# A decoder layer on one core: other places in SBUF for TensorE's operands, and an accumulation moved ahead of a row maximum

## The chip, the cores and the metric

The kernel runs on one core of a Trainium2 chip. The time is the device time of one execution in microseconds (us); of several executions the median counts.

## What is computed

A decoder layer for 8 sequences of 128 tokens, 512 features, all in float32. Cut to what matters:

```python
x = x + attn(layernorm(x))         # 32 query heads of 128 on 8 key/value heads; 16 cached blocks of 32 keys
                                   # and 128 new ones: 640 keys, rope, softmax, output projection 4096 -> 512
x = x + xattn(layernorm(x), ctx)   # rmsnorm, 32 heads of 128, keys and values from ctx (8 x 128 tokens),
                                   # score + position bias, mask, softmax, output projection 4096 -> 512
x = x + ffn(layernorm(x))          # gelu(x W1 + b1) W2 + b2, 512 -> 2048 -> 512
```

## The kernel before, in words

**Products.** A float32 product is made of three matmuls in the type float32r: each operand is split into a rounded part `_hi` (ScalarE copies, L485) and the rest `_lo` (VectorE or GpSimd subtract), and `mm3` (L1112 to L1116) adds hi x hi (L1114), hi weights x lo moving (L1115) and lo weights x hi moving (L1116). Every matmul loads its own weights. In the rows a matmul is written as output<-moving operand,weights. The trace has a row for a matmul (PE) and one for the load of its weights (PEld).

**Stages.** Three long loops follow one another, each over units of one head (or one 128-wide slice of the hidden layer) and one half of the 1024 tokens: 64 units of self-attention (`a_step`), 64 of cross-attention (`c_step`), 32 of the feed-forward part (`f_step`). Every engine runs the same list of units in an order written out by hand; semaphores tie them. The loads of the weights (SyncE) run two heads ahead.

**A unit n of self-attention on TensorE.** Scores of unit n+1 (L1179: weights q, moving K, 320 columns), queries of unit n+2 (12 products of 512 columns), then for each of 5 key tiles: four transposes of the probabilities (L1244: moving `ident`, weights `prob`), three matmuls of the output projection of unit n-1 (`a_out`: weights oT, moving wo) and three of probabilities times V (`pv`: weights V, moving pT). VectorE takes the row maxima, the low parts and the sums into `xacc` (L884).

**A unit n of cross-attention on TensorE** (L1341 to L1404), in this order: transposes of `xprob` (L1371); scores of unit n+1 (L1312, L1313: weights xq, moving xk, 256 columns); in two units of four (u mod 4 = 0, 3) a first tile of values (24 matmuls: weights cT, moving xwv, 256 columns); output product 0 of unit n-1 (`o(0)`: weights xoT, moving xwo); 12 of queries of unit n+2 (weights xwq, moving xT); in the same two units a second tile of values; `o(1)`; the product with xV (L1396, L1397: weights xV, moving xpT); 12 of keys of unit n+2 (weights xwk, moving cT); `o(2)`, `o(3)`. `o(i)` writes a bank that VectorE's accumulation i-1 (L884, `acc(i-1)`) must have emptied: `o(1)` waits for `acc(0)`.

**The same unit on VectorE** (L999 to L1049): low part of the transposed probabilities (L1010); `c_score` for unit n+1: two additions (L985, L987) and the row maximum (L990); in the two units with values a low part (L957); `acc(0)`; reciprocal (L1025); low part of the queries (L1028), which waits for ScalarE's xq_hi; factor (L1031); in the units with values the second low part; `acc(1)`; sum of the output halves (L1037); xoT_lo (L1042), which waits for ScalarE's xoT_hi; low part of the keys (L966), which waits for ScalarE's xk; `acc(2)`, `acc(3)`. ScalarE's exponentials (L631, four a unit) wait for the maximum, and its xq_hi stands behind them.

**Places.** A tensor's place is its first byte in each partition. Tensors are placed one behind the other in the order of their declaration (L50 to L137), each size rounded up to 32 bytes; a stage's tensors start again where the ones common to all end. Four names, of which the kernel reads nothing, only fill (`shift2`, `shift3`, `shift4`, 32 bytes each). All rows of the operands are a multiple of 512 bytes long or start at one, but for K (its second half starts 1280 bytes on). Places modulo 512 in the kernel before:

| operands | place before |
|---|---|
| xT, ident | 128 |
| K, q, wq, V, wo | 320 |
| prob, pT, oT, xwv | 384 |
| cT, xwk, xwq, xwo | 320 |
| xq, xk, xV, xprob, xpT, xoT | 384 |
| w1, w2 | 320 |
| hid_hi, hid_lo | 384 |

Of the kernel before, what the change touches and what calls it, by code (L numbers as in the profile page):

```python
# [13 lines left out]
P = 128  # L14
# [20 lines left out]
def decoder_layer(nc, x, ctxT, mask, fcos, fsin, wq, wk, wv, wo, kc, vc, bidx,  # L35
# [3 lines left out]
    with ExitStack() as ctx:  # L39
        def sb(stack, name, shape, dt=F32):  # L40
            return stack.enter_context(nc.sbuf_tensor(name, shape, dt))
# [14 lines left out]
        negmax = sb(ctx, "negmax", [P, 2, 4])  # L56
        rowsum = sb(ctx, "rowsum", [P, 2, 4])
        rinv = sb(ctx, "rinv", [P, 2, 4])
        sb(ctx, "shift2", [P, 8])


        with ExitStack() as ph:
            K_all = sb(ph, "K_all", [P, KB, NKV, BLOCK])
            V_all = sb(ph, "V_all", [P, KT, NKV * P])
            K_hi, K_lo = pair(ph, "K", [P, 2, T])
            q_hi, q_lo = pair(ph, "q", [P, 2, HALF])
            wq_raw = sb(ph, "wq_raw", [P, 2, C, P])
            wq_cos = sb(ph, "wq_cos", [P, C, P])
            wq_sin = sb(ph, "wq_sin", [P, C, P])
            wq_rot = sb(ph, "wq_rot", [P, C, P])  # L70
            wq_hi, wq_lo = pair(ph, "wq", [P, 2, C, P])
            V_hi, V_lo = pair(ph, "V", [P, 2, KT, P])
            wo_raw = sb(ph, "wo_raw", [P, 2, D])
            wo_hi, wo_lo = pair(ph, "wo", [P, 2, D])
            rope = sb(ph, "rope", [P, 2, P])
            ropeq = sb(ph, "ropeq", [P, 2, P])
            idx_sb = sb(ph, "idx_sb", [1, TOPK], I32)
            with ExitStack() as pro:
                kv_raw = sb(pro, "kv_raw", [P, 4, C, D])
                knew = sb(pro, "knew", [P, 3, D])  # L80
                xn1 = sb(pro, "xn1", [P, B, D])
                x0T = sb(pro, "x0T", [P, C, P])
            with ExitStack() as lo_:
                prob = sb(lo_, "prob", [P, 2, 4, T])
                pT_hi, pT_lo = pair(lo_, "pT", [P, KT, HALF])
                oT_hi, oT_lo = pair(lo_, "oT", [P, HALF])

                xwv_raw = sb(lo_, "xwv_raw", [P, C, 2 * P])
                xwv_hi, xwv_lo = pair(lo_, "xwv", [P, C, 2 * P])

        with ExitStack() as ph:

            cT_hi, cT_lo = pair(ph, "cT", [P, C, TOK])
            c_raw = sb(ph, "c_raw", [P, 2, TOK])

            xwk_raw = sb(ph, "xwk_raw", [P, 2, C, P])
            xwk_hi, xwk_lo = pair(ph, "xwk", [P, 2, C, P])
            xwq_raw = sb(ph, "xwq_raw", [P, 2, C, P])
            xwq_hi, xwq_lo = pair(ph, "xwq", [P, 2, C, P])
            bias_sb = sb(ph, "bias_sb", [P, 2, P])  # L100
            mask_sb = sb(ph, "mask_sb", [P, B, P], U8)
            negmask = sb(ph, "negmask", [P, B, P])
            lnw_sb = sb(ph, "lnw_sb", [P, D])

            xwo_raw = sb(ph, "xwo_raw", [P, 2, D])
            xwo_hi, xwo_lo = pair(ph, "xwo", [P, 2, D])
            anykey = sb(ph, "anykey", [P, B])
            sb(ph, "shift3", [P, 8])
            comb = sb(ph, "comb", [P, 2, 4, P])
            xq_hi, xq_lo = pair(ph, "xq", [P, 2, HALF])  # L110
            xk = sb(ph, "xk", [P, 2, 4, 2, P], F32R)
            xV_hi, xV_lo = pair(ph, "xV", [P, 2, 4, 2 * P])
            with ExitStack() as pro:
                xn2 = sb(pro, "xn2", [P, B, D])
            with ExitStack() as lo_:
                xprob = sb(lo_, "xprob", [P, 2, 4, P])
                xscore = sb(lo_, "xscore", [P, 2, 4, P])
                xpT = sb(lo_, "xpT", [P, 4, 2, P], F32R)
                xo = sb(lo_, "xo", [P, 2, 4, P])
                xoT_hi, xoT_lo = pair(lo_, "xoT", [P, 2, HALF])  # L120

        with ExitStack() as ph:

            w1_raw = sb(ph, "w1_raw", [P, 2, C, P])
            w1_hi, w1_lo = pair(ph, "w1", [P, 2, C, P])
            w2_raw = sb(ph, "w2_raw", [P, 2, D])
            w2_hi, w2_lo = pair(ph, "w2", [P, 2, D])
            b1_sb = sb(ph, "b1_sb", [P, 2])
            sb(ph, "shift4", [P, 8])
            b2_sb = sb(ph, "b2_sb", [P, D])  # L130
            hid = sb(ph, "hid", [P, 2, HALF])

            hid_hi, hid_lo = pair(ph, "hid", [P, 2, HALF])
            xn3 = sb(ph, "xn3", [P, B, D])
            yacc = sb(ph, "yacc", [P, B, D])
            finite = sb(ph, "finite", [P, B, D], I32)
            ysum = sb(ph, "ysum", [P, B, D])  # L137
# [11 lines left out]
        for p in (1, 2, 3):  # L149
# [17 lines left out]
        c = {n: sem("c_" + n) for n in (  # L167
            "qwhi", "qwlo", "kwhi", "kwlo", "vwhi", "vwlo", "owhi", "owlo", "comb", "S", "score", "max", "exp",
            "tr", "pThi", "pTlo", "pv", "ohi", "osum", "oThi", "oTlo", "q", "qhi", "qlo", "k", "khi", "klo", "v", "vhi", "vlo",
            "rinv", "wo", "y", "res")}  # L170
# [582 lines left out]
        def _(dve):  # L753
# [225 lines left out]
            xq_lo_evac(0, 1)  # L979
            ln_lo(2, 1)  # L980

            def c_score(n, slot, half):
                dve.wait_ge(c["S"], n + 1)
                dve.wait_ge(c["comb"], n + 1)
                v.tensor_tensor(xscore[:, slot], XS_bank[:, :, 0:P], comb[:, half], ALU.add).then_inc(c_s1, 1)  # L985
                dve.wait_ge(c_s1, n + 1)
                v.tensor_tensor(xscore[:, slot], XS_bank[:, :, P:2 * P], xscore[:, slot], ALU.add)\  # L987
                 .then_inc(c["score"], 1)
                dve.wait_ge(c["score"], n + 1)
                v.tensor_reduce(negmax[:, slot, :], xscore[:, slot], AX_X, ALU.max, negate=True)\  # L990
                 .then_inc(c["max"], 1)
# [7 lines left out]
            def c_step(it, u):  # L999
                n, k = it * 4 + u, u % 2  # L1000
                static = isinstance(n, int)
                more1, more2 = (not static or n + 1 < UNITS), (not static or n + 2 < UNITS)
                first = static and n == 0

                def acc(i):
                    if not first:
                        accumulate(c, n - 1, 1 - k, 1 - k, i, (XW_last if static and not more2 else XW_bank)[i], None)

                dve.wait_ge(c["pThi"], n + 1)
                v.tensor_tensor(xpT[:, :, 1, :], XT_bank.rearrange("p (t n) -> p t n", t=4), xpT[:, :, 0, :],  # L1010
                                ALU.subtract).then_inc(c["pTlo"], 1)
                if more1:
                    c_score(n + 1, 1 - k, 1 - k)
                vs = (u % 4 == 0 and not first) or (u % 4 == 3 and more1)
                if vs:
                    vhalf = 1 if u % 4 == 0 else 0
                    cnt = (it + u // 4) * 4 + (2 if vhalf else 4)
                    v_evac(vhalf, 0, cnt + 1)
                if not first:
                    dve.wait_ge(c["rinv"], n)  # L1020
                acc(0)
                if not static or n > 1:
                    dve.wait_ge(c["y"], 4 * n - 4)
                dve.wait_ge(c["exp"], 4 * n + 4)
                v.reciprocal(rinv[:, k, :], rowsum[:, k, :]).then_inc(c_r1, 1)  # L1025
                if more2:
                    dve.wait_ge(c["qhi"], n + 3)
                    v.tensor_tensor(xq_lo[:, k], XQ_bank, xq_hi[:, k], ALU.subtract).then_inc(c["qlo"], 1)  # L1028
                dve.wait_ge(c_r1, n + 1)

                v.tensor_tensor(rinv[:, k, :], rinv[:, k, :], anykey[:, 4 * k:4 * k + 4], ALU.mult)\  # L1031
                 .then_inc(c["rinv"], 1)
                if vs:
                    v_evac(vhalf, 1, cnt + 2)
                acc(1)
                dve.wait_ge(c["ohi"], n + 1)
                v.tensor_tensor(xo[:, 1], XO_bank[:, :, P:2 * P], xo[:, 0], ALU.add)\  # L1037
                 .then_inc(c["osum"], 1)
                if not more1:
                    acc(2)  # L1040
                dve.wait_ge(c["oThi"], n + 1)
                v.tensor_tensor(xoT_lo[:, k].rearrange("p (t n) -> p t n", t=4), xo[:, 1],  # L1042
                                xoT_hi[:, k].rearrange("p (t n) -> p t n", t=4),
                                ALU.subtract).then_inc(c["oTlo"], 1)
                if more2:
                    xk_lo_evac(k, n + 3)
                if more1:
                    acc(2)
                acc(3)  # L1049
# [467 lines left out]
```

## Time and profile before

| | |
|---|---|
| three runs | 2090.53, 2092.18, 2090.71 us; median 2090.71 |
| the profiled execution | 2089.98 us |
| its span, first to last instruction | 2088.0 us, 33806 instructions |
| granted TensorE clock, mean | 0.995 |

The span is what the profile's page and the trace cover; 1.98 us of the profiled execution lie outside it. A busy share is the time in which at least one instruction of the engine runs. The ends of TensorE's matmuls are modelled and overlap the next one's start, so the pace is read from the starts.

### The profile page before, as it was taken

How to read it: one execution, taken by the hardware profiler on the slowest of the kernel's cores; microseconds unless marked ns; L12 is line 12 of the kernel's file. 1: busy time of each engine (PE TensorE's matmuls, PEld its weight loads, DVE VectorE, ACT ScalarE, POOL GpSimd, SP SyncE). 2: the span in 40 equal slices, each digit the busy share in tenths (PEclk: the TensorE clock that was granted, in tenths of full speed). 3: DMA queues.
4: the chain of work that ended last, by engine and by line, in shares of the span. 5: the costliest groups of instructions: out<-in, count | busy, mean ns of one | idle time of the engine just before them, and what ended most of it. 6: DMA issues, size and time to landing. Idle time of an engine off the chain costs nothing.

```text
span 2088.0 us, 33806 instructions
## 1 busy us (share of the span) xinstructions
PE 2043.8 (98%) x11544; PEld 1768.8 (85%) x11544; DVE 1471.1 (70%) x2367; ACT 1012.9 (49%) x2230; POOL 530.7 (25%) x428
## 2 busy tenths in 40 slices
PE   8999999999999999999899999999999999989996
PEld 6888888888888888887788888888888888877885
DVE  6777777777777777777766666666666666677776
ACT  3555555555555555555544444444444444433331
POOL 2222212222122212222122222222222222223223
PEclk9999999999999999999999999999999999999998
DMA  7000000000000000011111111111111111011111
GB/s 233 21 21 21 21 11 20 20 20 11 19 20 20 15 15 20 15 55 32 47 43 44 43 43 43 43 43 43 43 38 37 37 43 43 23 36 27 49 48 48
DMA packets 44162, 76.90 MB, mean 37 GB/s; under 512 B 7378, under 2 KB 13650, under 8 KB 43602
## 3 DMA queue, kind: packets, MB, share of 16 engines
q1 hardware_dynamic: 44114, 76.25, 11.9%
q8 instruction: 32, 0.52, 0.1%
q14 instruction: 16, 0.13, 0.0%
HBM read 74.13 MB, written 2.10 MB: 37 GB/s over the span
## 4 chain that ended last, share of the span: by engine, by line
PE 93%; DVE 3%; ACT 2%; SPq 1%; issue 1%; DMA 0%; POOL 0%; DVEq 0%; ACTq 0%
PE bank L1114 23%; PE bank L1116 23%; PE bank L1115 23%; PE bank L1179 11%; PE bank L1244 7%; PE bank L1312 1%; PE bank L1396 1%; PE bank L1397 1%; PE bank L1313 1%; PE bank L1371 1%; PE bank L1169 0%; DVE xn L805 0%; SPq L214 0%; DVE xT_lo L811 0%; SPq L215 0%
## 5 line engine op out<-in xcount | busy, mean ns | idle before, releaser
L884 DVE SCALAR_TENSOR_TENSOR xacc<-bank,rinv,xacc 128x512 f32<-128x512 f32 x512 | 376.2, 746 | 71.4 <-PE bank L1116 71.0
L485 ACT ACTIVATE pT_hi<-bank 128x512 fp32r<-128x512 f32 x320 | 191.3, 599 | 213.0 <-PE bank L1244 213.0
L874 DVE TENSOR_REDUCE negmax<-bank 128x1 f32<-128x640 f32 x256 | 210.6, 822 | 46.6 <-PE bank L1179 39.1
L939 DVE TENSOR_TENSOR pT_lo<-bank,pT_hi 128x512 fp32r<-128x512 f32 x320 | 218.1, 682 | 2.4 <-ACT pT_hi L485 2.4
L537 ACT ACTIVATE prob<-bank,negmax 128x640 f32<-128x640 f32 x256 | 203.2, 794 | 24.5 <-DVE negmax L874 24.5
L1244 PE MATMUL bank<-ident,prob 128*128 128x128 f32 x1280 | 191.2, 272 | 0.0
L1244 PEld LDWEIGHTS bank<-ident,prob 128*128 128x128 f32 x1280 | 159.2, 140 | 19.5
L382 POOL TENSOR_TENSOR wo_lo<-wo_raw,wo_hi 128x512 fp32r<-128x512 f32 x32 | 42.1, 1315 | 413.4 <-ACT wo_hi L485 413.4
L631 ACT ACTIVATE xprob<-xscore,negmax 128x128 f32<-128x128 f32 x256 | 100.1, 394 | 95.0 <-DVE negmax L990 95.0
L1114 PE MATMUL bank<-xwv_hi,cT_hi 128*128 128x256 f32 x512 | 141.7, 277 | 1.4 <-DVE xV_lo L957 1.4
L1116 PE MATMUL bank<-xwv_hi,cT_lo 128*128 128x256 f32 x512 | 141.5, 276 | 0.0
L1115 PE MATMUL bank<-xwv_lo,cT_hi 128*128 128x256 f32 x512 | 141.4, 276 | 0.0
L1114 PE MATMUL bank<-pT_hi,V_hi 128*128 128x512 f32 x320 | 127.3, 398 | 2.5 <-DVE pT_lo L939 2.5
L382 POOL TENSOR_TENSOR xwo_lo<-xwo_raw,xwo_hi 128x512 fp32r<-128x512 f32 x32 | 41.3, 1290 | 346.5 <-ACT xwo_hi L485 346.5
L1116 PE MATMUL bank<-pT_hi,V_lo 128*128 128x512 f32 x320 | 126.8, 396 | 0.0
L1115 PE MATMUL bank<-pT_lo,V_hi 128*128 128x512 f32 x320 | 125.7, 393 | 0.0
L1179 PE MATMUL bank<-K_hi,q_hi 128*128 128x320 f32 x512 | 123.9, 323 | 1.0 <-ACT prob L537 1.0
L1114 PE MATMUL bank<-wo_hi,oT_hi 128*128 128x512 f32 x256 | 122.4, 478 | 2.0 <-DVE oT_lo L879 2.0
L1028 DVE TENSOR_TENSOR xq_lo<-bank,xq_hi 128x512 fp32r<-128x512 f32 x62 | 42.9, 692 | 108.3 <-ACT xq_hi L485 108.3
L1088 DVE TENSOR_TENSOR yacc<-bank,yacc 128x512 f32<-128x512 f32 x128 | 85.0, 685 | 47.0 <-PE bank L1116 46.8
L1179 PE MATMUL bank<-K_hi,q_lo 128*128 128x320 f32 x512 | 117.3, 310 | 0.0
L378 POOL TENSOR_TENSOR wq_lo<-wq_rot,wq_hi 128x512 fp32r<-128x512 f32 x32 | 41.7, 1302 | 293.7 <-ACT wq_hi L485 293.7
(172 smaller groups left out, 5754.3 us busy)
## 6 DMA issues: line engine op xcount, KB each, us to landing
wq_raw<-in_wq SPq DMA_DIRECT2D x32, 256.0 KB, 2.7
wo_raw<-in_wo SPq DMA_DIRECT2D x32, 256.0 KB, 2.7
xwv_raw<-in_xwv SPq DMA_DIRECT2D x16, 512.0 KB, 3.5
xwk_raw<-in_xwk SPq DMA_DIRECT2D x32, 256.0 KB, 3.6
xwq_raw<-in_xwq SPq DMA_DIRECT2D x32, 256.0 KB, 3.5
xwo_raw<-in_xwo SPq DMA_DIRECT2D x32, 256.0 KB, 2.7
w_raw<-in_w SPq DMA_DIRECT2D x32, 256.0 KB, 2.6
xacc<-in_x SPq DMA_DIRECT2D x8, 256.0 KB, 5.8
```

The source lines that it names most:

```text
L485: return s.activation(dst, src, ACT.Copy)
L537: s.activation(prob[:, slot, i, :].rearrange("p (a t) -> p a t", a=2), S_bank[i % 2], ACT.Exp, bias=negmax[:, slot, i:i + 1], scale=1.0, a ...
L631: s.activation(xprob[:, slot, i, :], xscore[:, slot, i, :], ACT.Exp, bias=negmax[:, slot, i:i + 1], scale=1.0, accum_out=rowsum[:, slot, i ...
L874: v.tensor_reduce(negmax[:, slot, i:i + 1], S_bank[i % 2], mybir.AxisListType.XY, ALU.max, negate=True).then_inc(a["max"], 1)
L884: v.scalar_tensor_tensor(xacc[:, 4 * half + i, :], M, rinv[:, k, i:i + 1], xacc[:, 4 * half + i, :], ALU.mult, ALU.add).then_inc(sems["y"], 1)
L939: v.tensor_tensor(pT_lo[:, j, :], T_bank[j % 2 if k == 0 else (j + 1) % 2], pT_hi[:, j, :], ALU.subtract).then_inc(a["pTlo"], 1)
L1088: v.tensor_tensor(yacc[:, t, :], Y_bank[i], yacc[:, t, :], ALU.add).then_inc(f["acc"], 1)
L1114: t.matmul(dst, w[0], m[0], start=start, stop=False)
L1115: t.matmul(dst, w[0], m[1], start=False, stop=False)
L1116: return t.matmul(dst, w[1], m[0], start=False, stop=stop)
L1179: last = t.matmul(S_bank[i % 2][:, hf, :], w[:, k, cols], K[m][:, ks, hf * TH:(hf + 1) * TH], start=(j == 0), stop=(j == 2))
L1244: last = t.transpose(T_bank[j % 2 if k == 0 else (j + 1) % 2][:, i * P:(i + 1) * P], prob[:, k, i, j * P:(j + 1) * P], ident[:, :])
```

## The change

Two edits. The first only moves tensors. `shift2` grows from 32 to 352 bytes, `shift1` (448 bytes) and `ahead3` (64 bytes) are new, `shift3` and `shift4` grow from 32 to 480 bytes. After it the places modulo 512 are:

| operands | before | after |
|---|---|---|
| xT, ident | 128 | 128 |
| K, q, wq, V, wo | 320 | 128 |
| prob, pT, oT | 384 | 128 |
| xwv | 384 | 192 |
| cT, xwk, xwq, xwo | 320 | 128 |
| xq, xk, xV, xprob, xpT, xoT | 384 | 128 |
| w1, w2 | 320 | 128 |
| hid_hi, hid_lo | 384 | 128 |

The second edit reorders VectorE in cross-attention: in the units without a tile of values (two of four) `acc(0)` with its wait for the factor stands between the second score addition and the row maximum, where it stood behind the maximum. In the units with values nothing moves.

```diff
-        sb(ctx, "shift2", [P, 8])
+        sb(ctx, "shift2", [P, 88])
...
             idx_sb = sb(ph, "idx_sb", [1, TOPK], I32)
+            sb(ph, "shift1", [P, 112])
...
+                sb(lo_, "ahead3", [P, 16])
                 xwv_raw = sb(lo_, "xwv_raw", [P, C, 2 * P])
...
-            sb(ph, "shift3", [P, 8])
+            sb(ph, "shift3", [P, 120])
...
-            sb(ph, "shift4", [P, 8])
+            sb(ph, "shift4", [P, 120])
...
-            def c_score(n, slot, half):
+            def c_score(n, slot, half, ahead=None):
...
                  .then_inc(c["score"], 1)
+                if ahead:
+                    ahead()
                 dve.wait_ge(c["score"], n + 1)
                 v.tensor_reduce(negmax[:, slot, :], xscore[:, slot], AX_X, ALU.max, negate=True)\
...
+                vs = (u % 4 == 0 and not first) or (u % 4 == 3 and more1)
+
+                def first_acc():
+                    if not first:
+                        dve.wait_ge(c["rinv"], n)
+                    acc(0)
+
                 if more1:
-                    c_score(n + 1, 1 - k, 1 - k)
-                vs = (u % 4 == 0 and not first) or (u % 4 == 3 and more1)
+                    c_score(n + 1, 1 - k, 1 - k, None if vs else first_acc)
                 if vs:
                     vhalf = 1 if u % 4 == 0 else 0
                     cnt = (it + u // 4) * 4 + (2 if vhalf else 4)
                     v_evac(vhalf, 0, cnt + 1)
-                if not first:
-                    dve.wait_ge(c["rinv"], n)
-                acc(0)
+                if vs or not more1:
+                    first_acc()
```

## Rows read from the trace of the kernel before

**Rows 1.** The page: busy time by engine; the chain that ended last, by engine.

```profile
PE 2043.8 (98%) x11544; PEld 1768.8 (85%) x11544; DVE 1471.1 (70%) x2367; ACT 1012.9 (49%) x2230; POOL 530.7 (25%) x428
...
PE 93%; DVE 3%; ACT 2%; SPq 1%; issue 1%; DMA 0%; POOL 0%; DVEq 0%; ACTq 0%
```

**Rows 2.** Busy time in stretches: stretch, us, engines in order, granted clock, DMA.

```profile
core 0: us, PE busy (x) PEld busy (x) DVE busy (x) ACT busy (x) POOL busy (x), PEclk, DMA share, GB/s
...
60.00:960.00 900.00, 899.72 (x5058) 787.82 (x5057) 665.54 (x1004) 498.27 (x1009) 198.85 (x179) 1.00 0.07 20
...
1030.00:1865.00 835.00, 829.48 (x4937) 726.01 (x4938) 548.97 (x938) 388.38 (x995) 232.07 (x170) 1.00 0.13 41
...
1900.00:2060.00 160.00, 160.00 (x690) 129.28 (x689) 118.14 (x145) 51.81 (x85) 38.31 (x28) 1.00 0.16 43
```

**Rows 3.** Timeline, PE, cross-attention keys, first and last of six: start us, us.

```profile
1102.28 0.39 PE L1114 MATMUL bank<-cT_hi,xwk_hi 128*128 128x512 f32 x1
...
1103.41 0.39 PE L1116 MATMUL bank<-cT_hi,xwk_lo 128*128 128x512 f32 x1
```

**Rows 4.** Timeline, PE: an output product's end, queries, first and last of seven.

```profile
1106.90 0.40 PE L1116 MATMUL bank<-xwo_hi,xoT_lo 128*128 128x512 f32 x1
1107.14 0.40 PE L1114 MATMUL bank<-xT_hi,xwq_hi 128*128 128x512 f32 x1
...
1108.54 0.40 PE L1114 MATMUL bank<-xT_hi,xwq_hi 128*128 128x512 f32 x1
```

**Rows 5.** Groups of PE, shapes apart: xcount | busy us, mean ns | idle before.

```profile
L1115 PE MATMUL bank<-pT_lo,V_hi 128*128 128x512 f32 x320 | 125.7, 393 | 0.0
...
L1115 PE MATMUL bank<-wo_lo,oT_hi 128*128 128x512 f32 x256 | 101.3, 396 | 0.0
L1115 PE MATMUL bank<-xwo_lo,xoT_hi 128*128 128x512 f32 x256 | 101.3, 396 | 0.0
...
L1115 PE MATMUL bank<-xT_lo,xwq_hi 128*128 128x512 f32 x256 | 100.8, 394 | 0.0
L1115 PE MATMUL bank<-xT_lo,wq_hi 128*128 128x512 f32 x256 | 100.4, 392 | 0.0
...
L1115 PE MATMUL bank<-cT_lo,xwk_hi 128*128 128x512 f32 x256 | 100.2, 391 | 0.0
...
L1115 PE MATMUL bank<-xT_lo,w_hi 128*128 128x512 f32 x128 | 50.5, 395 | 0.0
```

**Rows 6.** The same view: transposes, values and the product with xV.

```profile
L1244 PE MATMUL bank<-ident,prob 128*128 128x128 f32 x1280 | 191.2, 272 | 0.0
...
L1115 PE MATMUL bank<-xwv_lo,cT_hi 128*128 128x256 f32 x512 | 141.4, 276 | 0.0
...
L1396 PE MATMUL bank<-xpT,xV_hi 128*128 128x256 f32 x256 | 63.7, 282 | 0.0
```

**Rows 7.** Timelines of one cross-attention unit (u mod 4 = 2): VectorE, weight load, matmul.

```profile
1108.47 0.69 DVE L990 TENSOR_REDUCE negmax<-xscore 128x4 f32<-128x512 f32 x1
1109.07 0.74 DVE L884 SCALAR_TENSOR_TENSOR xacc<-bank,rinv,xacc 128x512 f32<-128x512 f32 x1
...
1109.87 0.19 PEld L1114 LDWEIGHTS bank<-xwo_hi,xoT_hi 128*128 128x128 f32 x1 [0.20 <-DVE xacc L884]
...
1109.94 0.43 PE L1114 MATMUL bank<-xwo_hi,xoT_hi 128*128 128x512 f32 x1
```

**Rows 8.** The unit's waits on VectorE (timeline); one of PEld (waits: total, times, longest).

```profile
1111.37 0.69 DVE L1028 TENSOR_TENSOR xq_lo<-bank,xq_hi 128x512 fp32r<-128x512 f32 x1 [1.47 <-ACT xq_hi L485]
...
1114.09 0.69 DVE L1042 TENSOR_TENSOR xoT_lo<-xo,xoT_hi 128x512 fp32r<-128x512 f32 x1 [0.70 <-ACT xoT_hi L485]
1115.21 0.69 DVE L966 TENSOR_TENSOR xk<-bank,xk 128x512 fp32r<-128x512 f32 x1 [0.43 <-ACT xk L485]
...
PEld bank L1114 <- DVE xacc L884: 5.5, 30, 0.2
```

**Rows 9.** Timeline of a self-attention unit: a low part and the load behind it.

```profile
399.55 0.68 DVE L939 TENSOR_TENSOR pT_lo<-bank,pT_hi 128x512 fp32r<-128x512 f32 x1
...
400.30 0.19 PEld L1114 LDWEIGHTS bank<-pT_hi,V_hi 128*128 128x128 f32 x1
```

## The prediction

> **What bounds the kernel now.** The page comes first: TensorE is busy for 98% of the span and is 93% of the chain that ended last [rows 1]. Busy time of overlapping matmuls can hide small waits, so the table by stretches is read next: in the three long loops (self-attention, cross-attention, feed-forward) TensorE is busy for 899.7 of 900, 829.5 of 835 and 160.0 of 160 us, at granted clock 1.00, while VectorE is busy for 66 to 74% [rows 2]. So the time of these 1895 us is the number of matmuls times the distance from the start of one to the start of the next. The timelines give that distance. Six products of the cross-attention keys start from 1102.28 to 1103.41 us, five steps of 0.226 us [rows 3]; seven products of the cross-attention queries of the same shape start from 1107.14 to 1108.54 us, six steps of 0.233 us [rows 4]. Nothing waits in either stretch. Work of one shape thus has two paces, 7 ns apart, and the mean duration of a row shows the same difference (0.39 and 0.40 us), for each matmul is drawn some 0.165 us past the start of the next. That is what lets me price the places from the groups of instructions: a nanosecond in the mean of a group is a nanosecond of pace.
>
> **Change A, the places.** No instruction is added or removed by the five fillers. What changes is where an operand stands modulo 512 bytes. While a matmul streams its moving operand, the weights of the next are loaded; what I compare is the place of the weights against that of the moving operand. In the kernel before, the keys have both at 320 (equal). The other groups of 512 columns have them 64 or 192 apart. After the change all of these are equal. I take the middle product (L1115) of each group, because it is never the first behind a wait, and its mean duration [rows 5], against the 391 ns of the keys:
> - probabilities times V (64 apart): 393 ns, +2, x960 (three products of 320) = 1.9 us
> - self-attention output projection (64): 396 ns, +5, x768 = 3.8 us
> - cross-attention output projection (64): 396 ns, +5, x768 = 3.8 us
> - cross-attention queries (192): 394 ns, +3, x768 = 2.3 us
> - self-attention queries (192): 392 ns, +1, x768 = 0.8 us
> - feed-forward, first product (192): 395 ns, +4, x384; the second (64) has the same 395 and the same count: 3.1 us together
> The sum is 15.7 us, all of it on the path, since TensorE is the path. The keys themselves gain nothing: equal before and after. The same holds for scores of self-attention (both operands shift alike), for the cross-attention scores and its value product (both at 384, then both at 128), and for the value projection (64 apart before and after).
>
> The unknown is bounded from both sides. From above: the keys begin each group slower and only then run at 0.226 us; twelve of them take 2.75 us, 0.229 us each. If every 512-column product (5568 of them) ran at 0.226, it would be 3 x 5568 = 16.7 us more, a gain of 32 us. From below: equal places may cost where the weight load covers the whole stream. The rows for 256 columns say so: the value projection (64 apart) takes 276 ns a product, the product with xV (equal) 282 ns [rows 6], 6 ns more. The operands that newly become equal and are that short are the transposes, identity against prob and xprob: 256 apart before, equal after. There are 1280 [rows 6], 256 (four in each of 64 units) and 96 (of the layer norms) of them. I take 0 for them: their moving operand has 128 columns, half of a value product's and as many as the weights, so a delay of the moving side has the most room there; that is an estimate, no row shows an equal transpose. The other end is 1632 x 6 ns = 9.8 us, kept for the range. All tensors stay at multiples of 64 bytes; VectorE, ScalarE, GpSimd and the DMAs get 0, since in the loops they end inside TensorE's busy time.
>
> **Change B, the accumulation ahead of the row maximum.** It concerns two of four units (u mod 4 = 1, 2), where no value tile is evacuated. In such a unit VectorE does the two score additions, then the maximum (1108.47, 0.69 us), then the first accumulation (1109.07 to 1109.81 us) [rows 7]. TensorE's second output product waits for that accumulation: its weight load starts at 1109.87 us after 0.20 us of waiting and its matmul lasts 0.43 instead of 0.40 us [rows 7]. That is 0.03 us of stall in one unit of four, 15 times: 0.5 us; in the other unit the load waits too but in time (30 waits, 5.5 us in all, mostly hidden [rows 8]). Instructions of VectorE with no wait between them overlap by 0.08 us (the accumulation starts before the maximum ends). After the change the accumulation therefore starts at about 1108.36, 0.08 before the second addition ends (some 0.03 us before 1108.47), and ends at 1109.10; its own input, the first output product, was done at 1107.3 [rows 4]. So 0.5 us goes.
>
> What is queued behind it moves back. The maximum ends at 1109.70 instead of 1109.16, +0.54 us. Behind it come ScalarE's four exponentials and xq_hi, and VectorE's xq_lo, which already waits 1.47 us for xq_hi [rows 8]: it moves by the same 0.54 to 1111.91. The factor, the second accumulation (ends 1113.3; TensorE asks for it at about 1114.1), the sum of the output halves and xoT_lo all go 0.54 later; xoT_lo then ends at 1115.32 instead of 1114.78 [rows 8]. There VectorE used to wait 0.43 us for xk [rows 8], which ScalarE makes only when TensorE's keys end at 1114.55. That idle time absorbs the shift: xk_lo starts at 1115.24 instead of 1115.21. TensorE needs xk_lo for the next scores, after the transposes, at about 1116.1; it is there at 1115.93. Nothing is lost, but the margin of 0.2 us is what comes next. VectorE and ScalarE then wait for TensorE nowhere in such a unit, so their chain is as long as the unit; if TensorE gets 0.1 us faster per unit (12 queries by 3 ns, 12 output products by 5), they may hold it back by up to that in 30 units, 3 us. Without B, A's gain in these units would be held at once by the accumulation. The transposes of the next unit need the exponentials 4 us later than they come. SyncE has no queue moved; GpSimd's mask sum waits for the second addition, which does not move.
>
> In self-attention the next margin is pT_lo, which ends at 400.23 us, 0.07 us before the weight load that waits for it starts [rows 9]. The load can be 0.12 us later still without moving its matmul, as the waits of 0.17 to 0.20 us of rows 8 cost 0 to 0.03 us. The gain per transposed tile is some six products by 2 to 5 ns, so it holds.
>
> **Sum.** 15.7 + 0.5 = 16.2 us off the profiled execution's 2089.98 us (span 2088.0, 1.98 us around it) gives 2073.8; the median of the three runs is 0.7 us above that execution, so 2074.5, and I write 2074.
>
> **A rule against it.** The rows show two paces for one shape, and I read places into that; the groups also differ in what runs before them. The Trainium skill, in "TensorE: Matmul & The Clock Gate", Part 2, says that the engine has two independent read ports, so that loading the next weights takes nothing from the running matmul. By that rule A is worth nothing. No row here separates the two readings; the 6 ns between two 256-column groups without any wait speaks against the rule.
>
> **Rivals.**
> 1. The places do nothing. The paces then come from each group's neighbours, and only B is left: 2090.7 - 0.5 = 2090.2 us. For it: pairs of one distance (64) have rows from 393 to 396 ns, and queries (192) 392 and 394. Against it: the constant 0.226 and 0.233 us inside two groups of the same loop. Chance 0.12.
> 2. Slower: equal places hurt. Place: the transposes, which take their weights for their whole length. Price: 6 ns as in rows 6, on 1632 of them, 9.8 us, and nothing gained on the 512-column groups because the keys' pace has another cause: 2090.7 + 9.8 - 0.5 = 2100 us. It decides from 16.2 us of loss, or with A's gain absent from 0.3 ns per transpose on. Chance 0.13.
> 3. Partly: A works in the long groups, but in the runs of three behind the transposes (self-attention's 1728 products) it does not settle, and VectorE holds back the cross-attention units. 16.2 - 5.7 - 3 = 7.5 us: 2083 us. Chance 0.2.
> My forecast has the remaining 0.55, with cases up to the 32 us.
>
> **Numbers.** A measurement of this kernel can tell 0.2%, 4.2 us. The forecast and rival 3 are faster (0.55 + 0.2 = 0.75), rival 1 is the same (0.12), rival 2 slower (0.13). The range goes down to 0.226 us for all 512-column products and B, 2090.7 - 32.4 - 0.5, so 2057, and up to rival 1 with one nanosecond on each transpose (1.6 us), so 2092; rival 2 is left out.
>
> **What would show it.** Right: L1115 rows of all 512-column groups at 389 to 391 ns; values still 276; transposes still 272; PEld L1114 no longer waiting for xacc; L990 starting behind L884 in two units of four; the three loops shorter by some 6, 7 and 3 us. Wrong: these means unmoved (rival 1), L1244 and L1371 at 275 ns or more (rival 2), new waits of PEld L1312 on VectorE's xk (rival 3).

## The result, and the profile after

The changed kernel takes 2089.51 us (median of 20 runs, 2086.05 to 2092.04) against 2092.02 us (20 runs, 2090.22 to 2096.63): a ratio of 0.9987, with an interval from 0.9981 to 0.9993. That is 2.5 us, inside the 0.2% that I called no change, where 16 us were forecast and a time this near to the kernel before had been given a chance of 0.12; the median lies inside the range, near its upper end. Its profiled execution took 2086.64 us, with a span of 2084.2 us against 2088.0, so the two traces differ by 3.8 us.

The page of the kernel after, its busy times and its chain that ended last, answers to [rows 1]:

```profile
span 2084.2 us, 33806 instructions
...
PE 2040.2 (98%) x11544; PEld 1778.5 (85%) x11544; DVE 1439.4 (69%) x2367; ACT 1003.3 (48%) x2230; POOL 544.2 (26%) x428
...
PE 92%; DVE 4%; ACT 2%; SPq 1%; issue 1%; DMA 0%; POOL 0%; DVEq 0%; ACTq 0%
```

TensorE is the bound as before. The three stretches of [rows 2] are filled as before, with a little more of the list of instructions in two of them: 5084 matmuls in the 900 us of self-attention (5058 before) and 707 in the 160 us of the feed-forward part (690 before). In the 835 us of cross-attention there are 4918 (4937 before). (A stretch's edge cuts units of different matmuls, and a few records can be missing, so the counts are a hint, not a measure.)

```profile
60.00:960.00 900.00, 899.83 (x5084) 790.96 (x5085) 668.57 (x1010) 500.12 (x1015) 201.31 (x181) 1.00 0.07 20
1030.00:1865.00 835.00, 830.22 (x4918) 732.68 (x4918) 539.34 (x935) 375.94 (x986) 231.50 (x170) 1.00 0.13 40
1900.00:2060.00 160.00, 160.00 (x707) 132.53 (x706) 94.18 (x150) 53.92 (x88) 52.73 (x29) 1.00 0.16 43
```

The measure is the distance from the start of one matmul to the start of the next, summed by group over the whole trace. By a loop I mean from here on the repeated part of each stage, over the same instructions in every kernel: 48 units of self-attention, 52 of cross-attention and 24 of the feed-forward part. The self-attention loop went from 708.8 to 705.2 us, the feed-forward loop from 133.9 to 130.6 us, and the cross-attention loop the wrong way, from 697.0 to 699.7 us. The middle products of [rows 5] and [rows 6] now read (groups of PE, shapes apart; L1115 is L1124 here, L1244 is L1253 and L1396 is L1405):

```profile
L1124 PE MATMUL bank<-pT_lo,V_hi 128*128 128x512 f32 x320 | 125.8, 393 | 0.0
...
L1124 PE MATMUL bank<-xwo_lo,xoT_hi 128*128 128x512 f32 x256 | 100.8, 394 | 0.0
...
L1124 PE MATMUL bank<-wo_lo,oT_hi 128*128 128x512 f32 x256 | 100.4, 392 | 0.0
...
L1124 PE MATMUL bank<-xT_lo,xwq_hi 128*128 128x512 f32 x256 | 99.7, 390 | 0.0
...
L1124 PE MATMUL bank<-xT_lo,w_hi 128*128 128x512 f32 x128 | 49.8, 389 | 0.0
...
L1124 PE MATMUL bank<-xwv_lo,cT_hi 128*128 128x256 f32 x512 | 142.9, 279 | 0.0
...
L1253 PE MATMUL bank<-ident,prob 128*128 128x128 f32 x1280 | 191.3, 272 | 0.0
```

Feed-forward (395 to 389 ns), cross-attention queries (394 to 390) and both output projections (396 to 392 and 394) came down, the value projection went up (276 to 279), the transposes stayed at 272. The table has it group by group: the mean distance in the loops in ns, and what the group gained over the whole span, beside the forecast.

| group (products) | before | after | forecast, us | measured, us |
|---|---|---|---|---|
| probabilities times V (960) | 232.7 | 230.7 | 1.9 | 1.7 |
| self-attention output (768) | 261.0 | 260.3 | 3.8 | 0.6 |
| cross-attention output, with change B (768) | 234.2 | 228.8 | 4.3 | 1.9 |
| cross-attention queries (768) | 231.6 | 228.0 | 2.3 | 2.8 |
| self-attention queries (768) | 229.2 | 228.2 | 0.8 | 0.9 |
| feed-forward, first product | 231.7 | 226.7 | 1.5 | 1.8 |
| feed-forward, second product | 233.3 | 226.7 | 1.5 | 2.4 |
| scores of self-attention (1536) | 151.0 | 149.9 | 0 | 1.6 |
| scores of cross-attention (512) | 129.7 | 128.4 | 0 | 0.7 |
| **value projection (1536)** | 113.3 | 117.9 | 0 | **-6.6** |
| **transposes of xprob (256), with the time before the scores** | 88.3 | 103.6 | 0 | **-3.7** |
| transposes of prob (1280) | 88.5 | 88.5 | 0 | -0.1 |
| product with xV (512) | 118.9 | 119.4 | 0 | -0.9 |

The remaining groups (the keys, and small transposes outside the loops) add 0.6 us, and with the terms unrounded the sum is 3.9 us. The cross-attention output gained 3.4 us in its loop and gave 1.5 us back outside it, most of it to the clock: behind the loop six of its products took 426 to 562 ns from start to start in the kernel before, thirteen took 426 to 565 in the kernel after, and all eight of the last product with xV came at 213 ns, which is 0.7 of that row's 0.9 us. The stretch from 1860 to 1890 us, before and after (granted clock 0.94 and 0.83):

```profile
1860.00:1890.00 30.00, 22.00 (x136) 18.42 (x135) 26.46 (x59) 9.78 (x23) 12.84 (x9) 0.94 0.07 20
```

```profile
1860.00:1890.00 30.00, 23.23 (x129) 19.75 (x130) 26.24 (x54) 8.05 (x15) 12.75 (x8) 0.83 0.06 18
```

So two losses of 10.3 us together, each costed at nothing, took some seven tenths of the gain of 14.4 us. They are the subject of the runs.

### The profile page after: what moved, and what is told of

Its sections match the earlier page's. It is cut to its first block, busy times and chain, and to the rows that moved or that the text cites. A ratio compares the mean times of both kernels' runs of the same rounds, so it can differ in the third digit from the quotient of the medians.

```text
span 2084.2 us, 33806 instructions
## 1 busy us (share of the span) xinstructions
PE 2040.2 (98%) x11544; PEld 1778.5 (85%) x11544; DVE 1439.4 (69%) x2367; ACT 1003.3 (48%) x2230; POOL 544.2 (26%) x428
## 4 chain that ended last, share of the span: by engine, by line
PE 92%; DVE 4%; ACT 2%; SPq 1%; issue 1%; DMA 0%; POOL 0%; DVEq 0%; ACTq 0%
PE bank L1123 23%; PE bank L1125 22%; PE bank L1124 22%; PE bank L1188 11%; PE bank L1253 7%; PE bank L1321 2%; PE bank L1406 1%; PE bank L1405 1%; PE bank L1322 1%; PE bank L1380 1%; PE bank L1178 0%; DVE xacc L886 0%; DVE xn L807 0%; SPq L216 0%; DVE xT_lo L813 0%
## 5 line engine op out<-in xcount | busy, mean ns | idle before, releaser
L1253 PE MATMUL bank<-ident,prob 128*128 128x128 f32 x1280 | 191.3, 272 | 0.0
L1253 PEld LDWEIGHTS bank<-ident,prob 128*128 128x128 f32 x1280 | 159.0, 140 | 18.4
L1124 PE MATMUL bank<-xwv_lo,cT_hi 128*128 128x256 f32 x512 | 142.9, 279 | 0.0
L1124 PE MATMUL bank<-pT_lo,V_hi 128*128 128x512 f32 x320 | 125.8, 393 | 0.0
L487 ACT ACTIVATE xV_hi<-bank 128x512 fp32r<-128x512 f32 x64 | 38.2, 598 | 168.4 <-PE bank L1125 168.4
```

The costliest lines, as they stand in the source:

```text
L487: return s.activation(dst, src, ACT.Copy)
L1124: t.matmul(dst, w[0], m[1], start=False, stop=False)
L1253: last = t.transpose(T_bank[j % 2 if k == 0 else (j + 1) % 2][:, i * P:(i + 1) * P], prob[:, k, i, j * P:(j + 1) * P], ident[:, :])
```

## The experiments

Three questions stood open after the two traces: which of the losses belongs to the places and which to the order (e1, e2, e7, e8); whether a place has a pace, or a distance between two places (e3, e4); and why the values slowed at a distance that was kept (e5, e6, e9, e10).

Every kernel ran beside the kernel before on its chip; the median of those runs was 2092.03 us for the first four experiments, 2091.79 for the next four and 2092.00 for the last two. Loop times are those of one trace each, over the same instructions, and one pass through a loop repeats within 0.03 us (53.61 or 53.62 us for four units of cross-attention in the kernel before); more than nine positions in ten repeat within 1 ns.

### The two parts apart

`e1_places_only` has the five fillers of the change and the old order of VectorE.

```diff
-                    c_score(n + 1, 1 - k, 1 - k, None if vs else first_acc)
+                    c_score(n + 1, 1 - k, 1 - k)
...
-                if vs or not more1:
-                    first_acc()
+                if not first:
+                    dve.wait_ge(c["rinv"], n)
+                acc(0)
```

> The new places, the old order of VectorE. The changed kernel's trace shows the pace of 512-column products at 227 ns in long runs, values 4.5 ns slower a product (6.5 us in all), and the scores of two units of four held by VectorE by 0.1 to 0.15 us (3.7 us). Theory P (the order causes the wait for VectorE): with the old order the holds before the scores vanish, the second output product's weight load waits for the accumulation instead, 0.1 us in two units of four, some 3 us; time within 3 us of the changed kernel's. Rival Q (VectorE holds the scores only because TensorE is faster, in either order): the holds stay and the waits for the accumulation come on top; 3 us slower than the changed kernel. Values at the slower pace in both.

Measured: 2092.84 us (12 runs), ratio 0.9995 (0.9985 to 1.0006); span 2084.6, that of its fastest execution (2086.72 us). Self-attention loop 705.2 and feed-forward loop 130.6 us, as after. In the cross-attention loop (700.6) the values stand at 117.9 ns, as after. The output products are back at 233.9 ns: TensorE's load again waits for the accumulation, and for longer than the 0.2 us at most and 5.5 us in all of [rows 8], since the products ahead of it are faster. One unit's load in the timeline, then the row of the waits on PEld in the stretch of cross-attention:

```profile
1106.20 0.19 PEld L1116 LDWEIGHTS bank<-xwo_hi,xoT_hi 128*128 128x128 f32 x1 [0.32 <-DVE xacc L886]
```

```profile
PEld bank L1116 <- DVE xacc L886: 9.0, 30, 0.3
```

The transposes are back at 88.3 ns: with the old order nothing holds the scores, so theory P holds and rival Q falls. With the new places, what the new order costs before the scores (3.2 us in the loop) it earns back at the output products, 3.2 us, and on the queries, 0.9 us. The two timed kernels (0.9995 and 0.9987) aren't told apart by their intervals.

`e2_order_only` has the new order and the places of before: the diff of the change without its fillers.

> The old places, the new order of VectorE. Theory P: the 0.5 us of stall at the second output product goes and the scores are hardly held, since TensorE runs at the old pace: 0.5 us faster than before. Rival Q: no hold at all, same number. Rival R (the order alone lets the low part of the keys come late): holds before the scores of 0.05 us or more in 30 units, 1.5 us or more, so 1 us slower than before. Paces of all groups as before.

Measured: 2095.21 us (12 runs), ratio 1.0012 (1.0004 to 1.0021); span 2094.1. The cross-attention loop went from 697.0 to 696.6 us, all of it on the output products (234.2 to 233.5 ns), and every other group of the three loops is within 0.3 ns of before. So B alone earns 0.4 us in the loop, where 0.5 was forecast for the whole, and the hold before the scores is absent, as forecast for B alone. The 6 us that this trace is longer than the one of before lie outside the loops: 3.9 at the start, 2.8 between the cross-attention and the feed-forward loop. The stretch from 0 to 60 us, before and then in this run (us, busy time of PE, PEld, DVE, ACT, POOL, granted clock, DMA):

```profile
0.00:60.00 60.00, 52.62 (x267) 40.60 (x268) 37.22 (x82) 23.32 (x51) 16.95 (x21) 0.97 0.65 212
```

```profile
0.00:60.00 60.00, 51.77 (x241) 38.83 (x242) 34.82 (x78) 21.16 (x45) 16.91 (x21) 0.89 0.65 212
```

At a granted clock of 0.89 instead of 0.97, with the lower of the two levels (1.2 GHz) for part of the stretch, TensorE got through 26 matmuls fewer. Why a kernel gets such a start was not explained; the runs below show it in faster kernels too. It is why a difference of 2 us between two medians is read here from the loops, where the granted clock is 1.00.

### Places or distances

`e3_after_plus64` and `e4_before_plus64` put 64 bytes in front of all tensors, in the kernel after and before:

```diff
+        sb(ctx, "shift0", [P, 16])
         xacc = sb(ctx, "xacc", [P, B, D])
```

> The changed kernel with 64 more bytes in front of all tensors: every distance between two operands stays, every place moves by 64. Theory D (only the distance of weights from the moving operand counts): all paces as in the changed kernel, values' mean 281 ns or so, time unchanged. Theory H (what counts is where moving operand and weights stand modulo 128, moving at 0 and weights at 64 being the fast case for values): values back to a mean of 276 ns, 6.5 us faster than the changed kernel; equal groups unmoved at 227 ns. Theory N (the slower values come from what runs beside or ahead of them): as theory D.

> The kernel before with 64 more bytes in front of all tensors: distances stay, places move by 64. Theory D or N: every group's mean as in the kernel before, same time. Theory H: values go from moving at 0, weights at 64 (modulo 128) to the opposite and slow from a mean of 276 to about 281 ns (1536 products, 6.9 us slower); output projections (moving 64, weights 0 before) take the place that the queries had and get 2 to 4 ns faster, queries 2 to 4 ns slower; in sum 5 to 8 us slower than before.

Measured: e3 2088.7 us, 0.9988 (0.9977 to 0.9998), span 2084.7, and each group at the pace of after, values at 117.9 ns included (the loops 705.4, 699.7, 130.6). e4 2092.45 us, 1.0 (0.9992 to 1.0009), span 2085.4, and the groups at the pace of before but for the first feed-forward product (231.7 to 230.0). So a shift of all places by 64 bytes leaves the paces, and what counts is how the places stand to one another (theory D; H, by which a place modulo 128 counts, falls). The one exception, 0.5 us in the feed-forward loop of e4 with every distance kept, no run explains. No other shift was tried, and none of the runs tests that 512 bytes is the period of the distances. The values did not slow because they moved to 192 or cT to 128.

### The value projection

`e5_values_equal` makes its distance nothing as well, by taking away a filler of the change.

```diff
-                sb(lo_, "ahead3", [P, 16])
```

> The changed kernel without the 64 bytes ahead of xwv: the value projection's operands equal, too. In the changed kernel a value matmul starts every 117.9 ns, in the kernel before every 113.3, both 64 apart. Theory E (equal places cost 256-column products as in the product with xV): 118 to 120 ns a product, loop time within 3 us of the changed kernel. Rival F (equal is the fast case once nothing interrupts a run, as for 512 columns): 113 to 114 ns, 6.5 us faster than the changed kernel.

Measured: 2090.41 us (one run), span 2088.0. The values got slower still: 119.8 ns, the cross-attention loop 701.9 us, and the group's middle product 283 ns (first of two rows below; 276 before, 279 after). A tile entered from the queries starts 114, 119, 120 ns apart and stays at 120. This is theory E: for 256 columns the equal place is the bad one, as [rows 6] had it for the product with xV (equal, at 118.9 ns from start to start).

`e6_entry` keeps the values 64 bytes apart but moves the other side: cT and xwk go to 64 and xwv to 128, so that the moving operand of the values stands where the moving operand of the scores does (128), as it was in the kernel before (384 and 384).

```diff
-        sb(ctx, "shift2", [P, 88])
+        sb(ctx, "shift2", [P, 72])
...
+            sb(ph, "lead0", [P, 16])
...
-                sb(lo_, "ahead3", [P, 16])
...
+            sb(ph, "lead2", [P, 16])
...
+            sb(ph, "lead3", [P, 16])
```

> The changed kernel with cT and xwk 64 bytes back (place 64) and xwv at 128: values stay 64 apart, keys stay equal, but the first weights of a run of values (cT) are now 64 behind the moving operands of what runs ahead of it (xk, xT at 128); in the changed kernel they were equal to them, in the kernel before 64 behind and 192 ahead. A run's pace has at least two stable levels. Theory G (which level a run takes is set by how it is entered): values back at 113.3 ns, 4.5 ns x 1536 = 6.9 us less, about 2083 us. Rival N (the slower values come from other engines' work, which is no other here): still 118 ns and the changed kernel's time.

Measured: 2088.25 us (11 runs), 0.9976 (0.9967 to 0.9985), span 2086.8. The mean of the values is 115.5 ns, and that is two levels. One loop body has two tiles of each kind; here are the first and last matmuls of a tile behind the scores and of one behind the queries (PE timeline, e6), and then the group's row in e5 and in e6:

```profile
1117.96 0.28 PE L1125 MATMUL bank<-xwv_hi,cT_hi 128*128 128x256 f32 x1
...
1120.57 0.28 PE L1127 MATMUL bank<-xwv_hi,cT_lo 128*128 128x256 f32 x1
...
1124.11 0.28 PE L1125 MATMUL bank<-xwv_hi,cT_hi 128*128 128x256 f32 x1
...
1126.82 0.28 PE L1127 MATMUL bank<-xwv_hi,cT_lo 128*128 128x256 f32 x1
```

```profile
L1123 PE MATMUL bank<-xwv_lo,cT_hi 128*128 128x256 f32 x512 | 144.9, 283 | 0.0
```

```profile
L1126 PE MATMUL bank<-xwv_lo,cT_hi 128*128 128x256 f32 x512 | 142.1, 278 | 0.0
```

Behind the scores 23 steps take 2.61 us, 113.5 ns each; behind the queries 2.71 us, 117.8 ns each. Same operands, same places, same clock, no wait: a tile keeps the level on which it was entered for all of its 24 matmuls. In the kernel before both kinds run at 113.3 ns, in the kernel after both at 118. So the distance alone doesn't set the pace of the values. Theory G holds for half of the tiles only: by it both should have come back, since cT stands 64 below what both groups in front of it move. And "64 apart before and after" was no ground for "unchanged". The loop came down to 696.8 us, 2.9 below after; 0.8 of that is a shorter hold before the scores (99.8 ns for 103.6 in the table's row), and the output products lost 0.9 (230.3 ns for 228.8).

`e9_values_minus128` and `e10_values_plus64` vary the distance from e8 (below), in which the weights cT stand 64 bytes below xwv: in e9 xwv stands at 192, 128 away; in e10 at 0, 64 away on the other side of cT.

```diff
@@ e9_values_minus128, against e8
+                sb(lo_, "ahead3", [P, 16])
@@ e10_values_plus64, against e8
+                sb(lo_, "ahead3", [P, 96])
```

> The kernel of e8 with xwv another 64 bytes on: value weights (cT) 128 behind the moving operand. In e6 and e8 a tile of values entered from the scores runs at 113.3 ns and one entered from the queries at 117.6. Theory G (two stable levels, set by the entry, as long as the distance allows both): another distance may allow the fast level alone, then 113.3 for both tiles and 3.3 us less than e8; or the slow one alone, then both at 118 and 3.3 us more. Rival F (the farther apart, the better): both fast.

> The kernel of e8 with xwv 64 bytes below cT: value weights 64 ahead of the moving operand. If only the size of the distance counts, the same two levels as e8 and its time. If the sign counts, one level for both tiles: as 512-column products 64 ahead had no pace below 231 ns in the kernel before, the slow one or slower is expected, 118 to 120 ns, 3 to 5 us more than e8.

Measured: e9 2087.94 us, 0.9979 (0.9969 to 0.999), values at 119.2 ns with an uneven pattern (behind the scores 117, 122, 120, 119, 115 ns and again), loop 699.6 us, 4.7 above e8; rival F falls. e10 2084.56 us (4 runs), 0.9955 (0.9938 to 0.9971), the two levels of e6 again (113.5 behind the scores, 117.7 behind the queries), loop 694.2 us, where 3 to 5 us more than e8 was expected if the sign counts. So 64 bytes on either side give the fast level behind the scores, and 128 are nearly as slow as none.

### The hold before the scores

In the kernel after, the last of VectorE's idle time in a unit without values is gone. The timelines of DVE, PE and PEld at the end of such a unit (u mod 4 = 2), with the transposes and the first score of the next:

```profile
1109.40 0.69 DVE L1051 TENSOR_TENSOR xoT_lo<-xo,xoT_hi 128x512 fp32r<-128x512 f32 x1 [0.70 <-ACT xoT_hi L487]
1110.01 0.68 DVE L968 TENSOR_TENSOR xk<-bank,xk 128x512 fp32r<-128x512 f32 x1
...
1110.33 0.60 PE L1380 MATMUL bank<-ident,xprob 128*128 128x128 f32 x4
...
1110.81 0.19 PEld L1321 LDWEIGHTS bank<-xk,xq_hi 128*128 128x128 f32 x1
1110.84 0.36 PE L1321 MATMUL bank<-xk,xq_hi 128*128 128x256 f32 x1
```

The low part of the keys follows xoT_lo at once, without the wait of 0.43 us of [rows 8], ends at 1110.69, and the load of the scores starts 0.12 behind it. From the start of the transposes to the start of the scores it takes 0.51 us. The wait view of the stretch has no PEld row for it, as a hold of 0.1 us behind the transposes shows as no idle engine; but the waits of VectorE for ScalarE's keys halved, from 61 units to 31 (kernel after, then e7 below):

```profile
DVE xk L968 <- ACT xk L487: 20.2, 31, 0.7
```

```profile
DVE xk L968 <- ACT xk L487: 32.7, 61, 0.7
```

That idle time is gone in e2 as well, where TensorE is slower and the scores aren't held. So the order uses up VectorE's idle time, and only a faster TensorE on top makes the hold. The same row in e2:

```profile
DVE xk L966 <- ACT xk L485: 20.3, 31, 0.7
```

`e7_late_acc1` is the kernel after with the second accumulation moved behind the sum of the output halves, in the units without values only.

```diff
-                acc(1)
+                if vs or not more1:
+                    acc(1)
                 dve.wait_ge(c["ohi"], n + 1)
                 v.tensor_tensor(xo[:, 1], XO_bank[:, :, P:2 * P], xo[:, 0], ALU.add)\
                  .then_inc(c["osum"], 1)
+                if not (vs or not more1):
+                    acc(1)
```

> The changed kernel with the second accumulation moved behind the sum of the output halves, in the two units of four without values, where VectorE idles 0.70 us for xoT_hi. Theory P (scores are held by VectorE's chain because the reordering made it as long as the unit): chain 0.7 us shorter, holds of 0.09 and 0.15 us before the scores gone, 3.7 us faster than the changed kernel, about 2086. Rival S (the hold is ScalarE's, which makes xk behind xoT_hi): the holds stay, same time. Rival T: the third output product now waits for the second accumulation, 0.1 to 0.3 us in 30 units, 3 to 9 us slower.

Measured: 2085.42 us (6 runs), ratio 0.9969 (0.9957 to 0.9981), an interval that just touches that of the changed kernel. The same place in this kernel (DVE, PE and PEld timelines):

```profile
1114.91 0.69 DVE L1054 TENSOR_TENSOR xoT_lo<-xo,xoT_hi 128x512 fp32r<-128x512 f32 x1
1115.98 0.69 DVE L968 TENSOR_TENSOR xk<-bank,xk 128x512 fp32r<-128x512 f32 x1 [0.38 <-ACT xk L487]
...
1116.52 0.60 PE L1383 MATMUL bank<-ident,xprob 128*128 128x128 f32 x4
...
1116.84 0.19 PEld L1324 LDWEIGHTS bank<-xk,xq_hi 128*128 128x128 f32 x1
1116.87 0.36 PE L1324 MATMUL bank<-xk,xq_hi 128*128 128x256 f32 x1
```

The idle time is back (0.38 us), and from the transposes to the scores it takes 0.35 us, 0.16 less. The distance from the last transpose to the first score, start to start, is 28 ns in each unit of this kernel and of the kernel before; in the kernel after it is some 123 and 178 ns where u mod 4 is 2 and 3. In 15 rounds of four units that is 15 x (95 + 150) = 3.7 us, the table's loss. The loop went from 699.7 to 696.6 us with every other group within 0.2 ns: theory P, and neither S (the hold stays) nor T (the third output product waits). Its span is nevertheless 2087.0 us, for its first 60 us were at a granted clock of 0.89 as in e2: the loops, and 6 runs against the kernel before, say faster; a span that holds one such start does not.

`e8_entry_late_acc1` joins the edits of e6 and e7.

> Both edits of the two runs before this one. Theories G and P: 6.9 + 3.7 = 10.6 us less than the changed kernel, 2079 us, 0.6% below the kernel before. If only one holds, that one's gain. If VectorE's chain becomes the bound again with faster values, less than the sum; units with values have 2 us of idle on VectorE, so the sum is expected.

Measured: 2083.99 us (5 runs, 2081.19 to 2085.39), ratio 0.9957 (0.9944 to 0.9971), span 2083.0; cross-attention loop 694.9 us, transposes 88.8 ns, values at the two levels of e6. Expected were 10.6 us less than the changed kernel; the loop gives 4.8, since the values came back for half of their tiles, the hold that e6 had already shortened can't be won twice, and the output products stay at 230.3 ns. With e10 (0.9955), from which it can't be told apart, it is the fastest of all the kernels here, about 8 us below the kernel before.

## Why the prediction was wrong, point by point

- **The bound and the measure** held: TensorE's pace is the time, and a nanosecond in a group's mean was a nanosecond of pace where nothing else moved (queries 394 to 390 in the rows, 231.6 to 228.0 in the distances).
- **Places set the pace** held against rival 1. e1 moves places alone and shortens the self-attention loop by 3.6 us and the feed-forward loop by 3.3 us, e2 moves none and shortens neither. The rule of the Trainium skill ("TensorE: Matmul & The Clock Gate", Part 2) that the two read ports are independent, so that loading the next weights takes nothing from the running matmul, does not agree with this: one shape runs at 226.7 or 233.3 ns by the places of its operands. For 512 columns all operands moved at once, though, and other engines' tensors with them; only for the values did the moving operand move by itself (e5, e9, e10).
- **The value projection, "64 apart before and after: nothing"**, is the step that failed first, by 6.6 us. The distance was kept, the pace was not. The rows showed only that this group was at 276 ns in the one surrounding it had; I carried the number into another one. In e6 two tiles with the same places run at 113.3 and 117.8 ns, one behind the scores and one behind the queries.
- **"Nothing is lost, but the margin of 0.2 us is what comes next"** failed by 3.7 us. For B alone it was right (e2: no hold). I had named the other draw on this slack myself, TensorE's own gain of 0.1 us a unit, and put the resulting 3 us into rival 3 instead of into the sum. B's 0.54 us and A's gain draw on the same idle 0.43 us and the same margin of VectorE, so they belonged together in one account.
- **The self-attention output at 3.8 us** measured 0.6. Two steps failed. The middle product was taken to stand for all three of its kind, and it doesn't: the mean distances of the run of three were 317, 235 and 231 ns before and are 316, 230 and 235 ns after, so what the middle one gained the third lost. (The queries' "constant" 0.233 us hid the same thing: by position their steps went from 229 to 235 ns.) And the +5 ns compared a run of three products behind transposes with a run of twelve: the V products that follow are at 231, 231 and 230 ns, not yet at 227. The first output product is long in both kernels. Only this far was rival 3 right on the runs of three; probabilities times V got their 1.7 of 1.9 us.
- **The cross-attention output and B, 4.3 us**: 3.4 us in the loop, of which e2 gives B 0.4 alone. The wait of PEld for xacc (30 times in [rows 8]) is gone from the waits of the kernel after, as forecast. With the places changed B is worth more, for the wait that it removes had grown from 5.5 to 9.0 us (e1); A's 3.8 us on this group would hardly have come without it (233.9 ns). Outside the loop 1.5 us were given back, mostly at the lower clock.
- **Undersized**: feed-forward 4.3 us for 3.1 (both to 226.7 ns, the pace of the keys' best stretch in [rows 3]), cross-attention queries 2.8 for 2.3. **Not seen**: both kinds of scores, 2.3 us together, which I had left out since their distance didn't change. It is the values' mistake with the other sign.
- **The transposes of prob** stayed at 88.5 ns and 272 ns in the row, so rival 2's mechanism is absent where I put it. But what its price was read from, 256-column products slowed by equal places, is real: e5.

In sum: forecast 16.2; 2.4 less on the output of cross-attention, 3.2 less on that of self-attention, 3.9 more on the other groups that gained, and losses of 6.6, 3.7, 0.9 and 0.1 us make 3.2 us, and with 0.6 from the small groups that is the 3.8 us of the spans. The nearest number was rival 1's (0.5 us, 2090.2), and by luck: e1 refutes its mechanism, and the small total is gains and losses that nearly cancel. The nearest mechanism was rival 3's (7.5 us), which had the hold and the runs of three, but not the values.

What stays open: why a 24-matmul tile keeps one of two levels. The runs show that the level depends on where in the unit the tile stands, behind the scores or behind the queries (e6), and, with its own distance kept, on the other places (before, after, e6). That the group in front is the cause is argued, not shown: the two tiles of e6 also differ in what the other engines do beside them. Which of the operands of the group in front would count was not tried, nor where in the chip the two operands meet.

## What to carry to other kernels

Where TensorE is the path and each matmul loads its own weights, measure the distance from start to start by position in the loop, not the mean of a row: runs of three, runs of twelve and the first product behind another group have paces of their own. Changing a place changes also groups whose own distance is kept (the scores of self-attention went from 151.0 to 149.9 ns), so price such an edit only by running it, and try the neighbours' places as well as the group's. And when an edit takes slack from an engine while another makes the path faster, add both to one account of that engine's unit before calling either free.

## What the runs showed of the hardware

- One shape, operands of one type, granted clock 1.00 and no wait: a product of 512 columns comes each 226.7 ns (feed-forward loop, kernel after) or each 233.3 ns (before), with its weights' place equal to its moving operand's modulo 512 bytes or 64 away from it. Moving all places by 64 bytes changes neither (e3, e4).
- The pace settles. Twelve keys that follow the product with xV in the kernel after, with equal places, start 0.24 us apart, then five times 0.23, then closer (PE timeline: first, second, seventh, last, and the output product behind them):

```profile
1106.22 0.40 PE L1123 MATMUL bank<-cT_hi,xwk_hi 128*128 128x512 f32 x1
1106.46 0.40 PE L1124 MATMUL bank<-cT_lo,xwk_hi 128*128 128x512 f32 x1
...
1107.61 0.39 PE L1123 MATMUL bank<-cT_hi,xwk_hi 128*128 128x512 f32 x1
...
1108.74 0.39 PE L1125 MATMUL bank<-cT_hi,xwk_lo 128*128 128x512 f32 x1
1108.97 0.39 PE L1123 MATMUL bank<-xwo_hi,xoT_hi 128*128 128x512 f32 x1
```

  The first six take 1.39 us, 0.232 each, the next six 1.36, 0.227 each.
- For 256 columns the order of the distances is another: 113.3 to 113.5 ns or 117.7 to 117.9 at 64 bytes (before, after, e6, e10), 119.2 at 128, 119.8 at none.
- The pieces at the lower clock outside the loops move a kernel's single span by up to 6 us (e2, e7) while its loops repeat to 0.2 us where the places stand to one another as they did (e2, e3). Between two medians of this kernel a difference of 2 us says little about an edit.
